# Masked attention with residual and layer norm on one core: attention five units ahead of where it stood, and blank products in TensorE's waits at both ends

## The reference

```python
q = heads(x @ Wq + bq)
k = heads(x @ Wk + bk)
v = heads(x @ Wv + bv)
scores = jnp.einsum('bhqd,bhkd->bhqk', q, k) * scale
scores = jnp.where(mask[:, None] == 0, -jnp.inf, scores)
attn = jax.nn.softmax(scores, axis=-1)
out = jnp.einsum('bhqk,bhkd->bhqd', attn, v)
out = out.transpose(0, 2, 1, 3).reshape(b, s, D_MODEL)
return out @ Wo + bo
# and around it
x = _layernorm(x + attention(x, adj, ...), axis=-1)
```

## Time and profile before

| | us |
|---|---|
| median of 3 runs | 904.38 (902.62 to 906.38) |
| profiled execution, its own time | 906.47 |
| its span, first to last instruction | 904.7 |
| PE busy | 870.5 (96%) |
| VectorE busy | 810.5 (90%) |
| ScalarE busy | 689.5 (76%) |
| GpSimd busy | 272.3 (30%) |

### The profile page before, as it was taken

How to read it: one execution, slowest core, us unless ns; L and a number is a source line. 1 busy time by engine, 2 the same in 40 slices (tenths; PEclk the granted TensorE clock), 3 DMA queues, 4 the chain that set the end, 5 groups by cost and what they waited for, 6 DMA issues and landing times.

```text
span 904.7 us, 32198 instructions
## 1 busy us (share of the span) xinstructions
PE 870.5 (96%) x11784; PEld 607.9 (67%) x11784; DVE 810.5 (90%) x3449; ACT 689.5 (76%) x1745; POOL 272.3 (30%) x386
## 2 busy tenths in 40 slices
PE   6989999999999999999999999999999999999954
PEld 4666667776667777666777666777766677766632
DVE  5779999999999999999999999999999999999983
ACT  5777778877788877787887778877778788777761
POOL 0113233332233332323333223333232333322222
PEclk9999999999999999999999999999999999999967
DMA  8267899879789988799887779898889998778773
GB/s 302 59 129 123 161 182 183 164 152 153 151 171 179 177 169 153 136 167 182 181 159 172 144 148 169 178 177 161 145 159 159 182 178 171 156 141 158 149 135 93
DMA packets 362414, 144.98 MB, mean 160 GB/s; under 512 B 340752, under 2 KB 344848, under 8 KB 361872
## 3 DMA queue, kind: packets, MB, share of 16 engines
q1 hardware_dynamic: 362256, 142.93, 81.6%
HBM read 42.21 MB, written 16.78 MB: 65 GB/s over the span
## 4 chain that ended last, share of the span: by engine, by line
PE 93%; DVE 4%; DMA 1%; issue 1%; ACT 0%; SPq 0%; POOL 0%; POOLq 0%; DVEq 0%
PE proj_ps L605 76%; PE score_ps L605 9%; PE av_ps L605 8%; DVE masked L492 1%; DVE p_pair L479 1%; DMA w_land<-weights 1%; DVE y L518 0%; DMA aT<-a_pair 0%; DVE stats L521 0%; DVE v_parts L465 0%; DVE a_pair L458 0%; ACT probs L407 0%; ACT p_pair L417 0%; SPq L253 0%; DVE inv_sum L501 0%
## 5 line engine op out<-in xcount | busy, mean ns | idle before, releaser
L407 ACT ACTIVATE probs<-masked,minus_max 128x128 f32<-128x128 f32 x1024 | 327.0, 390 | 167.2 <-DVE minus_max L492 166.3
L492 DVE CUSTOM_DVE_ANT_0 masked<-score_ps,mask 128x128 f32<-128x128 f32 x1024 | 237.4, 287 | 45.1 <-PE score_ps L605 39.8
L479 DVE SCALAR_TENSOR_TENSOR p_pair<-probs,p_pair 128x512 f16<-128x512 f32 x256 | 197.6, 772 | 1.3 <-ACT p_pair L417 1.0
L605 PE MATMUL proj_ps<-wo_hi,aT 128*128 128x512 f16 x512 | 166.3, 387 | 2.7 <-DMA aT<-a_pair 1.6
L417 ACT ACTIVATE p_pair<-probs 128x512 f16<-128x512 f32 x256 | 161.3, 630 | 8.1
L225 POOL TENSOR_TENSOR xT_lo<-xT_raw,xT_hi 128x512 f16<-128x512 f32 x60 | 69.9, 1165 | 317.0 <-ACT xT_hi L370 317.0
L605 PE MATMUL proj_ps<-xT_hi,wq_hi 128*128 128x256 f16 x512 | 141.7, 277 | 8.6 <-DVE wq_lo L573 7.6
L605 PE MATMUL proj_ps<-xT_lo,wq_hi 128*128 128x256 f16 x512 | 141.2, 276 | 0.0
L605 PE MATMUL proj_ps<-xT_hi,wq_lo 128*128 128x256 f16 x512 | 141.2, 276 | 0.0
L605 PE MATMUL proj_ps<-xT_hi,wk_hi 128*128 128x256 f16 x512 | 140.2, 274 | 0.0
L605 PE MATMUL proj_ps<-xT_hi,wk_lo 128*128 128x256 f16 x512 | 139.6, 273 | 0.0
(11 more groups left out here) (58 smaller groups left out, 1521.2 us busy)
## 6 DMA issues: line engine op xcount, KB each, us to landing
xT_raw<-x_cols SPq DMA_DIRECT2D x32, 512.0 KB, 4.5
x_in<-x_rows SPq DMA_DIRECT2D x32, 512.0 KB, 5.4
out<-y SPq DMA_DIRECT2D x64, 256.0 KB, 4.6
adj_in<-adj SPq DMA_DIRECT2D x32, 128.0 KB, 2.9
pT<-p_pair SPq DMA_TRANSPOSE x256, 3.4
w_land<-weights SPq DMA_DIRECT2D x2, 1024.0 KB, 7.5
w_land<-weights SPq DMA_DIRECT2D x4, 256.0 KB, 4.8
x_res<-weights SPq DMA_DIRECT2D x1, 1024.0 KB, 9.3
```

Of the source, the lines that this page charges most:

```text
L407: ins = act.activation(probs[s % 2][:, j * S:(j + 1) * S], masked[s % 2][:, j], ACT.Exp, bias=minus_max[s % 2][:, j:j + 1], scale=-1.0)
L479: dve.scalar_tensor_tensor(out=p_pair[s % NT][:, HW:2 * HW], in0=probs[s % 2][:], scalar=P_UP, in1=p_pair[s % NT][:, 0:HW], op0=ALU.mult, ...
L492: ins = dve.tensor_tensor_reduce(masked[s % 2][:, j], score_ps[j][:, s % HC], mask[par][:, s // KC], -EXP_SCALE, 3.0e38, ALU.add, ALU.min, ...
L605: return pe.matmul(dst, lhsT, rhs, start=first, stop=last)
```

## The change

`TASKS` is now Q, K, Q, K, V, V, Y, Y, with the halves of Q and K in turn, and Y of the second batch of the group before ahead of Y of the first batch of this one. A step of group g works for attention on units further ahead: scores 6, maximum 5, turning of the probabilities 4, attend 2, normalization 1. The loop runs from g = -1, a group that makes the first projections and begins attention on them. Scores of a group's first and third unit wait for the K half that they need. On VectorE the extra work of a step moves: `low_part_attn` to steps 1 and 3, `y_and_moments` to steps 7 and 0, `make_mask` to step 2. Wv's and Wo's parts are made inside groups -1 and 0. The semaphore increments that split two waits (`vector_goes`, `gpsimd_goes`, `sync_goes`) are gone. A tile `blank` of zeros, 128 x 256, is made by GpSimd at the start, and `run_idle` issues products of it: 36 before the first weights are there, and 8, 8, 8 and 20 in the last group.

The core of the difference:

```diff
 
-    TASKS = ((Q, 0), (Q, 1), (K, 0), (K, 1), (V, 0), (Y, 0), (V, 1), (Y, 1))
-    LAG = 3
-    RANK = {(Q, 0): 0, (Q, 1): 1, (K, 0): 2, (K, 1): 3, (V, 0): 4, (V, 1): 5}
+    TASKS = ((Q, 0), (K, 0), (Q, 1), (K, 1), (V, 0), (V, 1), (Y, 1), (Y, 0))
+
+    SCORED, MAXED, TURNED, ATTENDED, NORMED = 6, 5, 4, 2, 1
+    RANK = {t: n for n, t in enumerate(TASKS[:6])}
     N_SPLIT = len(RANK)
...
+    def at_work(g, s, ahead):
+
+        u = unit(g, s) + ahead
+        return [divmod(u, SLOTS)] if 0 <= u < NG * SLOTS else []
...
                 nxt = 1 - par
                 for s in range(SLOTS):
-                    masked_max(g, s, par)
-                    before, slot = back(g, s, 1)
-                    if exists(before):
-                        low_part_probs(before, slot)
-                    if s > 0 and TASKS[s - 1][0] != Y and has_next(g):
+                    for unit_g, t in at_work(g, s, MAXED):
+                        masked_max(unit_g, t, unit_g % 2)
+                    for unit_g, t in at_work(g, s, TURNED):
+                        low_part_probs(unit_g, t)
+                    if 1 <= s <= N_SPLIT and has_next(g):
                         low_part_bank(g + 1, *TASKS[s - 1], nxt)
-                    if s in (2, 4) and at_least(g, 1):
-                        low_part_attn(g - 1, s // 4)
-                    before, slot = back(g, s, LAG + 1)
-                    if exists(before):
-                        head_norm(before, slot)
-                    if s == 0 and at_least(g, 2):
-                        y_and_moments(g - 2, 1, par)
-                    if s == 6 and at_least(g, 1):
-                        y_and_moments(g - 1, 0, nxt)
-                    if s == 1 and not at_least(g, 1):
+                    if s == 1 and g >= 1:
+                        low_part_attn(g - 1, 1)
+                    if s == 3 and g >= 0:
+                        low_part_attn(g, 0)
+                    for unit_g, t in at_work(g, s, NORMED):
+                        head_norm(unit_g, t)
+                    if g == -1 and s == 2:
+                        low_part_weight("v", range(KC))
+                    if s == 2 and has_next(g):
+                        make_mask(g + 1, nxt)
+                    if g == -1 and s == SLOTS - 1:
                         dve.wait_ge(b_out_mm, 1)
                         dve.wait_ge(bo_loaded, 16)
                         dve.tensor_tensor(b_out[:], b_out_ps[:], b_out[:], ALU.add).then_inc(b_out_made, 1)
-                    if s == 5 and has_next(g):
-                        make_mask(g + 1, nxt, k + par)
+                    if g == 0 and s < 3:
+                        low_part_weight("o", ((0, 1), (2,), (3,))[s])
+                    if s == (0 if has_next(g) else 3) and g >= 1:
+                        y_and_moments(g - 1, 0, nxt)
+                    if s == SLOTS - 1 and g >= 1 and has_next(g):
+                        y_and_moments(g - 1, 1, nxt)
+                    if s == 5 and not has_next(g):
+                        y_and_moments(g - 1, 1, nxt)
...
-                    if s == 1 and at_least(g, 2):
+                    if s == 0 and g >= 2:
                         normalize(g - 2, 1)
-                    if s == 2:
-                        if not at_least(g, 1):
+                    if s == 1 and g >= 1 and has_next(g):
+                        normalize(g - 1, 0)
+                    if s == (2 if has_next(g) else 0) and g >= 0:
+                        if g == 0:
                             pool.wait_ge(b_out_made, 1)
-                        residual(g, 0, par, k)
-                    if s == 4:
-                        residual(g, 1, par, k)
-                    if s in (3, 6) and has_x_next2(g):
-                        low_part_x(pool, g + 2, (s - 3) // 3, par)
-                    if s == 7 and at_least(g, 1):
-                        normalize(g - 1, 0)
+                        residual(g, 0, par)
+                    if s == (4 if has_next(g) else 0) and g >= 0:
+                        residual(g, 1, par)
+                    if s in (3, 5) and has_x_next2(g):
+                        low_part_x(pool, g + 2, (s - 3) // 2, par)
...
+            def run_idle(dst, n):
+
+                for _ in range(n):
+                    mm(dst, blank[:, 0:P], blank[:], True, True)
...
-                if s == 0:
-                    pe.wait_ge(split_out, split_no(g, K, 1) + 1)
+                if b == 0 and c % 2 == 0:
+
+                    pe.wait_ge(split_out, split_no(g, K, c // 2) + 1)
...
-            def group(g, par, k):
-                nxt = 1 - par
+            def group(g, par):
                 for s in range(SLOTS):
-                    step_bank(g, s, par)
-                    before, slot = back(g, s, LAG)
-                    if not has_next(g) and s < SLOTS - 1:
-                        scores(g, s + 1, par)
-                    if exists(before):
-                        attend(before, slot, par if s >= LAG else nxt)
                     if has_next(g):
-                        if s < SLOTS - 1:
-                            scores(g, s + 1, par)
-                        else:
-                            scores(g + 1, 0, nxt)
-
-            pe.wait_ge(x_lo_done, 2)
-            for kind, i in RANK:
-                if kind != Q:
-                    pe.wait_ge(split_out, split_no(0, kind, i) - 1)
-                split_bank(0, kind, i, 0, fresh=i == 0, prologue=True)
-            pe.wait_ge(w_loaded["o"][0], 16)
-            pe.wait_ge(bias_made, 2)
-            for ki in range(KC):
-                ins = mm(b_out_ps[:], b_v_wide[:, ki], w_raw["o"][:, ki], ki == 0, ki == KC - 1)
-            ins.then_inc(b_out_mm, 1)
-            scores(0, 0, 0)
-            all_groups(group)
-            attend(LAST, SLOTS - 3, LAST % 2)
-            attend(LAST, SLOTS - 2, LAST % 2)
-            attend(LAST, SLOTS - 1, LAST % 2)
-
-            y_bank(LAST, 0)
+                        step_bank(g, s, par)
+                        for unit_g, t in at_work(g, s, ATTENDED):
+                            attend(unit_g, t, unit_g % 2)
+                        for unit_g, t in at_work(g, s, SCORED):
+                            scores(unit_g, t, unit_g % 2)
+                        continue
+                    for unit_g, t in at_work(g, s, SCORED):
+                        scores(unit_g, t, unit_g % 2)
+                    if s == 4:
+                        step_bank(g, 6, par)
+                    if s in (2, 3):
+
+                        pe.wait_ge(max_done, NG * SLOTS)
+                        run_idle(score_ps[0][:, 0:2], 8)
+                    for unit_g, t in at_work(g, s, ATTENDED):
+                        attend(unit_g, t, unit_g % 2)
+
+            pe.wait_ge(blank_made, 1)
+            run_idle(score_ps[0][:, 0:2], 36)
+            for g in range(-1, NG):
+                group(g, g % 2)
+            run_idle(score_ps[0][:, 0:2], 8)
+            step_bank(LAST, 7, LAST % 2)
             pe.wait_ge(y_summed, batch(LAST - 1, 1) + 1)
+            run_idle(proj_ps[bank_of(Y, 1)][:, 0:TOK], 20)
             y_bank(LAST, 1)
```

More of the change, by code:

```diff
@@ L88, in wait @@
     def wait(eng, sem, value):
[L90 removed]
+        if value > 0:
             eng.wait_ge(sem, value)
[L93 to L94 removed]
     def has_next(g):
[L97 removed]
+        return g < LAST
     def has_x_next2(g):
[L100 to L111 removed]
+        return g < LAST - 1
+    def at_work(g, s, ahead):
+        u = unit(g, s) + ahead
+        return [divmod(u, SLOTS)] if 0 <= u < NG * SLOTS else []
     with ExitStack() as ctx:
```

278 lines of the change are left out of this document (120 added, 158 removed).

## The result

| | before | after |
|---|---|---|
| median of 4 runs, us | 904.49 | 933.66 |
| lowest and highest | 902.62, 906.38 | 933.28, 935.12 |
| ratio, 95% interval | | 1.0326 (1.0301 to 1.0350) |
| profiled execution, its span | 906.47, 904.7 | 935.12, 933.3 |

A forecast was written before the change was run, and what follows sets the result against it. TensorE (PE), busy 870.5 of 904.7 us, was taken to bound the kernel. Head 61.5 + middle 860.4 + tail 31 gave a 952.9 span against 904.7, hence 952 us predicted, range 892 to 962.

The forecast's parts named there:

- The mechanism: Middle: GpSimd's x_res starts 0.04 ahead of VectorE's low attn, holds it, and K's banks come late for scores.
- the signs named beforehand: Groups 28.7 apart, scores waiting for kT_lo about 1.2 and 0.7, low attn 1 us or more, PE busy about 94%.
- The removed semaphore increments cost VectorE and ScalarE nothing that shows: Whole kernel: claimed no gain on these engines; on GpSimd normalization perhaps about 0.1 earlier.
- The middle: 30 groups between head and tail: 28.68 us each instead of 26.73, so 860.4 against 802.0 before.
- The head: Stretch before the first complete group: ends at 61.5, 4.9 later than before; bounds 55.4 and 64.
- tail: Last group to the end: 31 us against 46.1 before; 34 with the clock low throughout, 28 if it never falls.
- The three waits: PE waits in a middle group: 1.17 for K's first bank, 0.09 for Q's second, 0.69 for K's second; together 1.95.
- VectorE's pieces 0.1 shorter each without their increments: Middle, step 1: x_res misses low attn, the middle stays nearly unchanged, measured 895.5; chance 0.27.
- The rival in which VectorE wins the collision: Middle, step 1: low attn goes first by 0.04, x_res waits; 0.92 a group lost, 922; chance 0.17.
- the one of the clock falling in the middle: Middle: each group's 1.2 wait lowers PE's clock once, 1.6 more a group, 990; chance 0.05.
- the step 1 collision: Middle: low attn waits out x_res to 11.45, VectorE's step 2 starts at 11.85, PE waits 1.17.

The follow-up runs named there:

- run 1: Kernel after, plus one wait on GpSimd putting a group's first x_res behind VectorE's low part of attention in step 1: 906.87 us, ratio 1.002.
- run 8: Kernel after with attention five units ahead instead of six, and the first x_res behind step 1's low part of attention: 901.92 us, ratio 0.997.
- run 5: run 1 with GpSimd's low half of the next xT also waiting for step 3's low part of attention: 913.06 us, ratio 1.009.
- run 3: Kernel after with all eight semaphore self-increments put back (VectorE, GpSimd, SyncE): 954.62 us, ratio 1.056.
- Run 11: Kernel after with only VectorE's two self-increments put back, ahead of the maxima and of bn_aggr: 955.01 us, ratio 1.055.
- run 4: Kernel after without any blank product, the tile and its waits kept: 932.08 us, ratio 1.030.
- run 2: Kernel after with attention five units ahead instead of six, batch 0's attn parts in step 4: 921.77 us, ratio 1.018.
- run 9: run 8 with SyncE's load of the next group's x_in moved from step 1 to step 5: 897.47 us, ratio 0.992.

## Why the prediction was right, and where its sizes were off

- **The mechanism.** x_res passes the low part of attention by 0.09 us (I had 0.04), holds it to 1.72, and kT_lo is late for scores of its own step. Shown by run 1, which moves only GpSimd's start and takes 1.04 of 1.15 per group away, and by run 8, which adds the missing slack for K and gets the whole. Of the signs named beforehand the long low part of attention, the waits for kT_lo and VectorE's lag in step 2 are there; the groups are 27.9 apart and not 28.7, and PE is busy for 96% of the middle and not 94%. That GpSimd would be first was in part luck: the working had it by 0.04, less than its own pieces were off. The Trainium skill, "SBUF — State Buffer", section "SBUF: two separate sides", has the port pair as a lock held to the end of an instruction. The trace after agrees: 1.72 at 434.92, and in run 5 again 1.74 at 433.69.
- **"The removed semaphore increments cost VectorE and ScalarE nothing that shows"** is the step that failed. I took VectorE's pieces of y's steps from the earlier trace rows, 3.66 each, with the increments in them. In the kernel after they are 3.44 (429.24 to 432.68): bn_aggr follows the start of the statistics by 0.73 and not 0.87, the maxima follow bn_aggr by 0.12 and not 0.21. GpSimd's normalization follows bn_aggr and moves along, so the collision stays, but all of it comes earlier against PE. The first wait is 0.54, with the increments 1.25 (run 3), 0.71 more: VectorE starts step 7 0.30 behind PE there and 0.12 here (0.18), two y steps are 0.46 longer, the hold 0.07. Run 11 puts the price of VectorE's two increments at 28.49 - 27.85 = 0.64 us a group, 19 us in all; all eight are 0.72 (run 3), 21.6 us.
- **The middle**, 833.5 instead of 860.4. Of the 26.9, 21.6 are the increments, 3.3 the distance from my 28.68 to run 3's 28.57, and 2.0 the distance from 30 groups of 27.85 to the measured middle. The head and tail were 4.4 and 2.9 longer than forecast, so the errors partly cancel: the span is 933.3 where the sum was 952.9. The range of 892 to 962 took in faster kernels too; that the time lies in it proves little beside the rows.
- **The three waits.** I had 1.17, 0.09 and 0.69; measured 0.54, 0 and 0.47, in sum 1.0 of the 1.15 (by the queue's own waits, those of PEld, 31.2 us in 26.9 groups, it is 1.16). One delay was missed: the maxima of step 3 start 0.17 behind the mask's end. The chain has the third of their three waits there, as an instruction of the queue (L470 is the wait for the mask):

```profile
439.62 0.42 DVE mask L512
...
440.07 0.05 DVEq L470
...
440.20 0.29 DVE masked L472
```

- **The rival "VectorE's pieces 0.1 shorter each without their increments"** had the right cause: the two y pieces got 0.22 shorter each. It was wrong in what follows from it: VectorE came about 0.6 earlier into step 1 than in run 3, still entered step 2 1.26 behind PE, and the middle wasn't free. The rival in which VectorE wins the collision and the one of the clock falling in the middle are out: x_res is first by 0.08 to 0.10 in the 26 groups, and the granted clock is 1.00 from 100 to 850 us.
- **The head**, 65.9 instead of 61.5. Two banks ran at the low clock behind waits for b_out (1.31) and for v_parts (0.80), 4.45 instead of 2.7 each, 3.5 of the 4.4. I priced this in the head of before and did not look for it behind the new waits. I also misread the place there: ahead of the bank of 4.34 PE was idle for 0.82 and for 0.80, with 16 score products between, and not for two stretches over 2 us.
- **The tail**, 33.9 instead of 31. I had the last maximum end 6.1 behind the stage's start; it began at 908.82, 9.4 behind, and ended 10.4 behind. Ahead of it on VectorE stand p_pair, which had to wait for ScalarE until 905.79, and the low part of attention, held by x_res to 1.67. The blanks of steps 2 and 3, which I took to be hidden behind the exponentials, are on the chain with 3.6 (run 4). The tail is only 2.9 longer all the same, so what came behind was shorter than I had it.

Left open: why the clock falls in the head in some executions and not in others with nearly the same waits there (it fell for both banks in after and in runs 5 and 11, for one in run 4, for none in runs 1 to 3, 8 and 9), and what scatters run 1's times over 10 us.

## What to carry to other kernels

Where two engines share a way to memory, follow them through the steps by start times and ask who is first; if the answer hangs on less than 0.1 us, order them by a wait, and check what the one that waits will meet next. Read the price of an edit at the engine that sets the pace after it: an instruction worth nothing under TensorE's cover was worth 0.64 us per group once VectorE led. A deeper software pipeline must leave a step between a producer's last part and its first use, or a small delay of the producer can be paid in full, as the step 1 collision was.

## What the runs showed of the hardware

- A 128x512 instruction of VectorE with both inputs in SBUF, 0.68 us by itself, that was wanted 0.02 to 0.10 behind the start of GpSimd's x_res ended 0.53 to 0.56 after x_res did, at 1.72 to 1.79 (after and runs 2, 3 and 11, nearly each group). The other way round x_res, 1.27 by itself, took 1.72 behind a p_pair (441.58).
- A self-increment of a semaphore on VectorE between a wait and the next instruction exposes time: bn_aggr starts 0.17 after the statistics' end with it (438.25, run 3), 0.04 after it without (432.56 against 431.83 + 0.69).
- The maxima with a third wait, the one for the mask, start 0.17 behind the mask's end, 27 times between 100 and 850 us. That an instruction reads what the one before it wrote isn't enough for that: bn_aggr does so too, with two waits, and starts 0.04 behind.
- Nine transpositions by DMA took 6.5 to 8.2 us where the median is 3.6, issued behind a 512 KB load and a 256 KB store (run 8); with the load four steps later none of the probabilities' took over 5.6 (run 9).
- A bank behind a wait of 0.80 to 1.31 us in the head took 4.34 to 4.45 or 2.76 to 2.78 in kernels that are nearly alike there; waits of 0.5 us, twice a group, never brought the clock down in the middle.
